# A 12-block transformer kernel with its instruction order written out by hand: new order, new counts of constant products, waits and weight loads moved

## The chip, the cores and the metric

The kernel runs on one core of one Trainium2 chip. The time is device time in microseconds (us) of one execution. The engines are PE (TensorE, matmuls; its weight loads are listed as PEld), DVE (VectorE), ACT (ScalarE), POOL (GpSimd) and SP (SyncE, which only waits and issues DMAs here). Each engine runs its own instructions in order; engines signal one another by semaphores.

## What is computed

Tokens x are 64 sequences of 64 rows by 128 columns; a context is 64 sequences of 128 rows by 96 columns. Four layers each add three blocks to x, every one on a normalised copy of x:

```
x = x + _L0_xattn_ref(_layernorm(x), ctx_768, ...)     # L0x: cosine scores against the context
x = x + _L0_attn_ref(_layernorm(x), ...)               # L0a: linear attention and a GELU MLP
x = x + _L0_ffn_ref(_layernorm(x), ...)                # L0f: 16 experts, 4 picked
x = x + _L1_xattn_ref(ctx_768, _layernorm(x), mask..)  # L1x: attention to context and latents
x = x + _L1_attn_ref(_layernorm(x), ...)               # L1a: 16 heads, rotary positions
x = x + _L1_ffn_ref(_layernorm(x), ...)                # L1f: MLP with 8 LoRA experts
...                                                    # L2x, L2a, L2f, L3x, L3a, L3f
```

L2x and L3x are attention with 16 heads to the context, L2a linear attention, L2f latent attention and 8 experts, L3a a gated linear attention and an MLP, L3f 8 experts of which 2 are picked, and a shared one.

## The kernel before

The tokens stay in SBUF (x_held, 32 tiles of 128 rows). A job is one block on a group of 4 tiles (2 tiles in L1x and L2f). Two contexts, each with its own 4 PSUM banks, semaphores and SBUF rooms, work through a list of jobs each (`PLAN`); each has one main job, and beside it the early part (norm, context tiles) of its next one.

Each block is written as Python generators, one for each engine (`pe_L2x`, `dve_L2x`, ...); what stands between two `yield`s is a step. `ORDER` is one long string that says in which order the steps are written out, and so the order of every engine's instructions. A lower-case letter is a step of context 0, an upper-case one of context 1: p, c, m, n are steps of PE; a, b, k, x, y of ACT; v, r, d, w, z of DVE; g, l of POOL; q, s of SP. A digit in front of a PE step is a number of constant products: `pe_warm` (line 456) writes as many products of two constants into a PSUM bank that is free at that point, and nobody reads them. `write_out` goes through the string. After each step it looks whether both contexts have written out their last job of the block three back; then it writes a wait of SP for those jobs (line 3048) and the DMA of the next block's weights (line 3009), since there are three weight rooms. All DMAs (weights, context tiles on line 518 and 1133, the experts' combination weights on lines 821 and 836) are on SP's queue.

Steps that the change touches:

- `j.free(v)` is DVE's wait for the end ("done") of its context's job before. In most blocks the first DVE step is this wait, and for a block's first job a memset.
- `pe_context` (L2x and L3x) projects the context to keys (line 1856) and values (line 1860), turns the normalised x and projects the queries (line 1870). Its last step only waits: for the queries (q_ready), the values in SBUF (va) and the keys, one plane for each lane (kx). PE's scores follow in `pe_waves` (L1a, L3x; line 1559) or in L2x's lanes (line 1953), which have those waits too.
- `dve_route_L3f` has a step that waits for e_low, which is written by the step before it.

Of the kernel before, what the change touches and what calls it, by code (L numbers as in the profile page):

```python
# [19 lines left out]
SLOTS = 3  # L20
# [761 lines left out]
def dve_L0a(nc, j):  # L782
    v, m, x = nc.vector, j.m, j.x
    yield
    j.free(v)
    if j.first:
        v.tensor_copy(m["va"][:, :, :, D], bcast(j.c["parity"][:, 0:2], 1, j.tiles))
# [522 lines left out]
def dve_L1x(nc, j):  # L1310
    v, m, x, psum = nc.vector, j.m, j.x, j.psum
    keys = SC + S
    yield
    j.free(v)
    if j.first:
        v.memset(m["vl"][64:P], 0.0)
        v.memset(m["plT"][64:P], 0.0)
    yield
    j.begin(v)
# [169 lines left out]
def dve_L1f(nc, j):  # L1489
    v, m, x, psum = nc.vector, j.m, j.x, j.psum  # L1490
    yield
    j.free(v)
    if j.first:
        v.memset(m["pickT"][:], 0.0)
# [100 lines left out]
def pe_waves(nc, j, keys):  # L1595
# [149 lines left out]
def pe_L1a(nc, j):  # L1745
# [17 lines left out]
    t.wait_ge(*j.at("va", 1))  # L1763
    t.wait_ge(*j.at("kx", 2))
    t.wait_ge(*j.at("qx", 1))
# [46 lines left out]
def dve_L1a(nc, j):  # L1812
    v, m, x, psum = nc.vector, j.m, j.x, j.psum
    yield
    j.free(v)
    if j.first:
        v.memset(m["va"][:, :, :, WIDTH], 1.0)
        v.memset(m["top"][:], 0.0)
# [30 lines left out]
def pe_context(nc, j):  # L1849
# [21 lines left out]
    yield  # L1871
    t.wait_ge(*j.at("q_ready", 1))
    t.wait_ge(*j.at("va", 1))
    t.wait_ge(*j.at("kx", 2))
# [17 lines left out]
def dve_context(nc, j):  # L1892
    v, m, x, psum = nc.vector, j.m, j.x, j.psum
    yield
    j.free(v)
    if j.first:
        v.memset(m["va"][:, :, :, WIDTH], 1.0)
        if "top" in m:
            v.memset(m["top"][:], 0.0)
# [127 lines left out]
def dve_L2x(nc, j):  # L2027
    v, m, x, psum = nc.vector, j.m, j.x, j.psum
    yield
    j.free(v)  # L2030
    if j.first:
        v.memset(m["va"][:, :, :, WIDTH], 1.0)
# [47 lines left out]
def pe_L3x(nc, j):  # L2080
    t, m, psum = nc.tensor, j.m, j.psum
    yield from pe_context(nc, j)
    t.wait_ge(*j.at("qx", 1))
# [79 lines left out]
def dve_L2a(nc, j):  # L2163
    v, m = nc.vector, j.m
    yield
    j.free(v)
    if j.first:
        v.tensor_copy(m["va"][:, :, :, D], bcast(j.c["parity"][:, 0:2], 1, j.tiles))
    yield from dve_linear(nc, j, j.c["same8"], j.c["head8"], 16)
    yield  # L2170
    dve_project(nc, j, 3)
# [278 lines left out]
def dve_L2f(nc, j):  # L2450
    v, m, x, psum = nc.vector, j.m, j.x, j.psum
    tok = j.tok
    yield
    j.free(v)
    if j.first:
        v.memset(m["va"][:, :, 16], 1.0)
# [218 lines left out]
def dve_L3a(nc, j):  # L2675
    v, m, x, psum = nc.vector, j.m, j.x, j.psum
    yield
    j.free(v)
    yield
# [104 lines left out]
def dve_route_L3f(nc, j):  # L2784
# [10 lines left out]
    yield  # L2795
    v.wait_ge(*j.at("e_low", 1))
# [3 lines left out]
def sp_L3f(nc, j):  # L2800
# [41 lines left out]
    "VVVVd4ppgGaapVGpppaakPAppkPPPDvvdDddvpAAalPpAAvvaavaPvPPPpVVVdKPAK4PVvAVAVApvVvvv4PvVPvvgVVv8pVVVa2pVVgGpppDDVDaaPppaaLD"
    "kAKppvPPvpPaAApdddlGApappaPvPAPPPVdbpvrrVrpapparvPAppPPPPparrrrrrrrrrrrrrrBrvvcAAbpapRRRRRRRvpssppPkVVsssPRRAaPPPpAaVggg"
    "PAPRvRvVVRRRRcccPgAggPcccggccPARRRRVvRpCBaPPpSSdDddDDpppPAbrrLSSaSvDpGpaKapvrrrvrrrrGGpaGpCCvrrrrrrVVCGGppCCGrrrrCCaGCVr"
    "lp1PpcAbadDvvDDpssssLPaBPsAppPPPgggVDvPaAAPVRVPAPPPRRVRRRkAccPpRRRRRRRRVRRRRRRvgAPPgVPgCccccggccBASSSSSPvpPapGpdpGaAbCpC"
# [185 lines left out]
def write_out(core, flows, last, load_weights):  # L3031
# [57 lines left out]
```

## Time and profile before

| | us |
|---|---|
| median of 3 runs (lowest, highest) | 2873.68 (2862.74, 2876.07) |
| span of the profiled execution, first to last instruction | 2859.1 |
| PE busy in it | 2483.8 |
| DVE, ACT, POOL busy | 1723.1, 1393.0, 782.2 |
| constant products on PE | 231.3, in 828 |
| TensorE clock granted, mean of full | 0.941 |

The profile gives the span of its execution and no total of its own. Busy times are a union over instructions; an engine that is not busy waits, or is between instructions. The granted clock is 1.00 at 2.4 GHz and 0.50 at 1.2 GHz, and a stretch's number is the mean over both.

### The profile page before, as it was taken

The page shows a single profiled execution, that of the slowest core. Times are in us where ns is not written, and L with a number is a line of the kernel's source. Part 1 is how long each engine was busy: PE and PEld are TensorE (multiplying, and loading weights), DVE is VectorE, ACT ScalarE, POOL GpSimd, SP SyncE. Part 2 cuts the span into 40 slices and gives each one's busy share as a digit, 9 for nine tenths or more (in the row PEclk, how much of TensorE's full clock was granted, in tenths as well). Part 3 has the DMA queues.
Part 4 walks back from the last instruction along what each step waited for, and adds up shares of the span by engine and source line. Part 5 has one row for each costly group of instructions (what it writes and reads, how often), then busy time and mean ns, then how long its engine had stood idle before and what let it go on. Part 6 is the DMA issues. An engine that isn't in the chain of part 4 may idle for free.

```text
span 2859.1 us, 63716 instructions
## 1 busy us (share of the span) xinstructions
PE 2483.8 (87%) x27260; PEld 1654.6 (58%) x27260; DVE 1723.1 (60%) x4680; ACT 1393.0 (49%) x2375; POOL 782.2 (27%) x684
## 2 busy tenths in 40 slices
PE   5899898887888899888998888788879888899999
PEld 3565566565555455455676666666545555566666
DVE  5766666656665657777676666555546555554533
ACT  3665345665443237676754344443334545654332
POOL 3322444543121231111012222221110022235444
PEclk9999999998889999999999898988979999899999
DMA  3001342000000001000000000000020000022133
GB/s 114 13 1 42 84 97 57 17 17 7 3 2 6 1 17 38 12 13 1 10 14 17 17 17 17 24 22 15 10 68 7 7 1 2 1 58 84 53 93 100
DMA packets 50459, 84.25 MB, mean 29 GB/s; under 512 B 9536, under 2 KB 24768, under 8 KB 49792
## 3 DMA queue, kind: packets, MB, share of 16 engines
q1 hardware_dynamic: 50176, 80.18, 10.2%
q8 instruction: 214, 3.51, 0.5%
q14 instruction: 69, 0.57, 0.1%
HBM read 77.54 MB, written 2.62 MB: 28 GB/s over the span
## 4 chain that ended last, share of the span: by engine, by line
PE 60%; DVE 17%; ACT 10%; issue 6%; POOL 5%; DMA 1%; SPq 0%; DVEq 0%; POOLq 0%; ACTq 0%
PE psum L917 5%; PE psum L875 4%; PE psum L879 4%; PE psum L456 3%; PE psum L1569 3%; PE psum L448 3%; PE psum L1559 2%; PE psum L1961 2%; PE psum L1953 2%; PE psum L1656 1%; POOL c_L3f_h L864 1%; DVE c_L3x_most L1698 1%; PE psum L2307 1%; PE psum L1856 1%; PE psum L1413 1%
## 5 line engine op out<-in xcount | busy, mean ns | idle before, releaser
L456 PE MATMUL psum<-halves_held 128*128 128x512 bf16 x828 | 231.3, 395 | 2.9 <-DVE c_L2x_p L2064 1.3
L907 DVE TENSOR_TENSOR c_L3f_h<-c_L3f_h,psum 128x512 f32<-128x512 f32 (+1 forms) x112 | 76.1, 685 | 115.5 <-PE psum L879 87.4
L864 POOL TENSOR_TENSOR c_L3f_h<-c_L3f_h,c_L3f_spread 128x512 f32<-128x512 f32 x96 | 121.5, 1299 | 85.9 <-DMA c_L3f_spread<-scratch 72.1
L456 PEld LDWEIGHTS psum<-halves_held 128*128 128x128 bf16 x828 | 77.1, 101 | 86.4 <-issue 31.2
L893 ACT ACTIVATE c_L3f_h<-psum 128x512 f32<-128x512 f32 (+1 forms) x112 | 65.2, 595 | 122.0 <-PE psum L875 99.5
L917 PEld LDWEIGHTS psum<-weights,c_L3f_h 128*128 128x128 f32 (+1 forms) x896 | 107.3, 193 | 17.8 <-issue 15.5
L917 PE MATMUL psum<-weights,c_L3f_h 128*128 128x128 f32 (+1 forms) x896 | 110.2, 278 | 0.2
L879 PE MATMUL psum<-c_L3f_xT,weights 128*128 128x512 f32 x208 | 106.1, 597 | 0.0
L875 PE MATMUL psum<-c_L3f_xT,weights 128*128 128x512 f32 x208 | 105.4, 596 | 0.0
L2058 DVE TENSOR_REDUCE c_L2x_mx<-psum 128x8 f32<-128x1024 f32 x64 | 77.6, 1219 | 43.3 <-PE psum L1953 42.9
L864 POOL TENSOR_TENSOR c_L0f_h<-c_L0f_h,c_L0f_spread 128x512 f32<-128x512 f32 x64 | 80.2, 1286 | 70.6 <-DMA c_L0f_spread<-scratch 59.1
L1698 DVE TENSOR_REDUCE c_L3x_most<-psum 128x16 f32<-128x2048 f32 x32 | 73.3, 2291 | 40.2 <-PE psum L1559 40.2
L1569 PE MATMUL psum<-c_L3x_qx,c_L3x_kT 32*128 32x256 f32 x512 | 77.6, 422 | 17.2 <-DVE c_L3x_most L1698 10.3
L2064 DVE SCALAR_TENSOR_TENSOR c_L2x_p<-psum,c_L2x_mx 128x1024 f32<-128x1024 f32 x64 | 77.7, 1220 | 1.3
L1997 ACT ACTIVATE c_L2x_p<-c_L2x_p 128x1024 f32<-128x1024 f32 x64 | 67.7, 1058 | 20.6 <-DVE c_L2x_p L2064 20.5
L1370 DVE TENSOR_TENSOR x_held<-x_held,psum 128x512 f32<-128x512 f32 (+1 forms) x48 | 28.6, 595 | 78.5 <-PE psum L2097 39.7
L1678 ACT ACTIVATE c_L3x_pT<-psum 128x1024 f32<-128x1024 f32 x64 | 62.7, 1020 | 26.0 <-PE psum L1591 25.7
L1953 PE MATMUL psum<-c_L2x_kx,c_L2x_qT 32*64 32x512 f32 x512 | 65.2, 625 | 11.5 <-DVE c_L2x_va L2039 6.9
L2002 ACT COPY c_L2x_pT<-psum 128x1024 f32<-128x1024 f32 x64 | 64.4, 1008 | 18.2 <-PE psum L1961 17.9
L1961 PE MATMUL psum<-constants_held,c_L2x_p 128*128 128x128 f32 x512 | 68.0, 276 | 5.5 <-ACT c_L2x_p L1999 5.3
L441 POOL TENSOR_TENSOR c_L3a_norm_rstd<-c_L3a_norm_rstd,constants_held 128x4 f32<-128x4 f32 x24 | 25.3, 1061 | 171.3 <-DVE c_L3a_norm_rstd L432 136.7
L917 PEld LDWEIGHTS psum<-weights,c_L0f_h 128*128 128x128 f32 x512 | 64.0, 203 | 13.8 <-POOL c_L0f_h L864 7.3
(645 smaller groups left out, 6822.0 us busy)
## 6 DMA issues: line engine op xcount, KB each, us to landing
c_L0f_spread<-scratch SPq DMA_DIRECT2D x64, 256.0 KB, 5.5
c_L3f_spread<-scratch SPq DMA_DIRECT2D x32, 512.0 KB, 5.6
c_L2f_spread<-scratch SPq DMA_DIRECT2D x64, 128.0 KB, 3.1
c_L3f_spread<-scratch SPq DMA_DIRECT2D x64, 128.0 KB, 5.9
c_L0x_ctxT<-ctxT SPq DMA_DIRECT2D x8, 384.0 KB, 7.6
c_L1x_ctx<-ctx SPq DMA_DIRECT2D x16, 192.0 KB, 2.4
c_L2x_ctxT<-ctxT SPq DMA_DIRECT2D x8, 384.0 KB, 3.9
c_L3x_ctxT<-ctxT SPq DMA_DIRECT2D x8, 384.0 KB, 4.0
```

Of the source, the lines that this page charges most:

```text
L448: put = nc.tensor.transpose(j.psum[0:width, bank, t * P:(t + 1) * P], x[:, t, :], j.c["ident"])
L456: nc.tensor.matmul(j.psum[:, bank, :], j.half["ident"], j.half["take"], start=True, stop=True)
L864: nc.gpsimd.tensor_tensor(h, h, j.m["spread"][:, f, :], ALU.mult).then_inc(*j.up("mixed"))
L875: t.matmul(psum[:, 1 + 2 * f % 3, 0:j.tok], j.weight("gate")[:, cols], m["xT"][:], start=True, stop=True).then_inc(*j.up("gate"))
L879: t.matmul(psum[:, 1 + (2 * f + 1) % 3, 0:j.tok], j.weight("up")[:, cols], m["xT"][:], start=True, stop=True).then_inc(*j.up("inner"))
L917: put = nc.tensor.matmul(j.psum[:, 0, k * P:(k + 1) * P], j.m["h"][rows, f, k * P:(k + 1) * P], j.weight("down")[rows, f * P:(f + 1) * P], ...
L1569: nc.tensor.matmul(j.psum[rows, g, at:at + 256].rearrange("p (j q) -> p j q", j=QUAD), j.m["kT"][f, s * keys:(s + 1) * keys], j.m["qx"][f, ...
L1698: put = v.tensor_reduce(m["most"][:, u, :].rearrange("p (g j) -> p g j", j=QUAD), psum[:, :, u * QUAD * keys:(u + 1) * QUAD * keys].rearra ...
L1953: put = t.matmul(psum[64 * r:64 * r + 64, g, :].rearrange("p (j k) -> p j k", j=QUAD), m["qT"][f, s * S:(s + 1) * S], m["kx"][f, :, s * SC ...
L1961: put = t.transpose(psum[:, n // 4, (n % 4) * P:(n % 4 + 1) * P], m["p"][:, n * P:(n + 1) * P], j.c["ident"])
L2058: v.tensor_reduce(mx, s, AX, ALU.max).then_inc(*j.up(lane_name("max", h)))
L2064: v.scalar_tensor_tensor(p, s, -limit, bcast(mx, 2, SC), ALU.max, ALU.subtract).then_inc(*j.up(lane_name("low", h)))
```

## The change

Steps that hold only a wait are gone or joined to the step that needs them, the waits of `pe_context` and `pe_L1a` now stand in `pe_waves` ahead of the first scores, a "+" in the order says where a weight load is written out, and the order with its digits is another one. PLAN, the arithmetic and the tiles are as before.

```diff
 def dve_L0x(nc, j):
     v, m, x = nc.vector, j.m, j.x
-    yield
-    j.free(v)
     if j.first:
+        yield
+        j.free(v)
         v.memset(m["tT"][64:P], 0.0)
...
@@ def pe_waves
         if w:
             pe_warm(nc, j, 2)
             t.wait_ge(*j.at("att", w))
+        else:
+            if tiles == 1:
+                t.wait_ge(*j.at("q_ready", 1))
+            t.wait_ge(*j.at("va", 1))
+            t.wait_ge(*j.at("kx", 2))
+            t.wait_ge(*j.at("qx", 1))
         pe_scores(nc, j, w, keys)
...
@@ def pe_L1a
     yield
-    t.wait_ge(*j.at("va", 1))
-    t.wait_ge(*j.at("kx", 2))
-    t.wait_ge(*j.at("qx", 1))
     yield from pe_waves(nc, j, S)
...
@@ def pe_context
     t.matmul(psum[:, 1, :], j.weight("wq"), m["xT"][:], start=True, stop=True).then_inc(*j.up("queries"))
-    yield
-    t.wait_ge(*j.at("q_ready", 1))
-    t.wait_ge(*j.at("va", 1))
-    t.wait_ge(*j.at("kx", 2))
...
@@ def dve_route_L3f
-    yield
-    v.wait_ge(*j.at("e_low", 1))
     yield from dve_weigh(nc, j)
...
 ORDER = (
-    "QVDDDdLdDdldKkqqdvddlDDdDkppLDaaKgPpaPgpAGppAvvavPAGPPvvPVvdVddlpagpAaVVdVpakgppQqQPDVDDLDPAApvvKGavvvPAPPGPVVAdddlVppag"
+    "dddlQqPADdkdDDLDdpapapKPaDDvdDVggLGlpppvvAaPAPGPPvvdvVVkQqqppaaAVVDVdgpaKgpppPPvvadvdAAPAGlGPPPvvdkdDDVppDVdAaapapgpgpVd"
...
@@ def write_out
-        if loaded < len(BLOCKS) and all(flow.finished > ends.get(loaded - SLOTS, -1) for flow, ends in zip(flows, last)):
+        if letter == "+":
             for flow, ends in zip(flows, last):
                 if loaded - SLOTS in ends:
                     core.nc.sync.wait_ge(flow.context.sem("done"), ends[loaded - SLOTS] + 1)
             load_weights(loaded)
             loaded += 1
+            continue
...
```

The same joining of `yield` and `j.free(v)` with `if j.first` is made in dve_L0a, dve_L1x (which keeps the wait in its second step), dve_L1f, dve_L1a, dve_context, dve_L2x, dve_L2a and dve_L2f; dve_L3a loses its wait, and pe_L3x its wait for qx, which is now in pe_waves. The first of the order's 71 lines stands above, old and new.

## Rows read from the trace of the kernel before

**Rows 1.** The page: span, busy time by engine, share of the ending chain.
```profile
span 2859.1 us, 63716 instructions
PE 2483.8 (87%) x27260; PEld 1654.6 (58%) x27260; DVE 1723.1 (60%) x4680; ACT 1393.0 (49%) x2375; POOL 782.2 (27%) x684
...
PE 60%; DVE 17%; ACT 10%; issue 6%; POOL 5%; DMA 1%; SPq 0%; DVEq 0%; POOLq 0%; ACTq 0%
```

**Rows 2.** Busy time by stretch: L0a, L1x, L1a, L2x, L2f, L3x/L3a, L3f.
```profile
core 0: us, PE busy (x) PEld busy (x) DVE busy (x) ACT busy (x) POOL busy (x), PEclk, DMA share, GB/s
120.00:290.00 170.00, 161.16 (x899) 107.08 (x898) 107.45 (x383) 102.81 (x170) 42.07 (x38) 1.00 0.10 23
450.00:660.00 210.00, 172.76 (x1705) 125.35 (x1704) 131.33 (x401) 134.24 (x338) 101.01 (x74) 0.98 0.07 20
660.00:930.00 270.00, 220.48 (x4163) 143.36 (x4159) 169.75 (x425) 118.93 (x197) 53.46 (x43) 0.88 0.02 4
1090.00:1420.00 330.00, 294.50 (x3684) 174.01 (x3683) 238.37 (x435) 240.87 (x316) 40.81 (x25) 0.97 0.03 8
1550.00:2080.00 530.00, 446.58 (x7076) 335.52 (x7075) 320.17 (x925) 214.59 (x373) 124.44 (x155) 0.90 0.06 17
2080.00:2500.00 420.00, 355.13 (x4488) 224.88 (x4487) 222.90 (x554) 206.82 (x319) 72.84 (x60) 0.91 0.05 15
2500.00:2859.00 359.00, 348.30 (x2048) 230.16 (x2046) 161.28 (x425) 143.85 (x238) 153.91 (x122) 0.99 0.28 77
```

**Rows 3.** Line 456: its group, its durations (min/median/max ns), and in L0a.
```profile
L456 PE MATMUL psum<-halves_held 128*128 128x512 bf16 x828 | 231.3, 395 | 2.9 <-DVE c_L2x_p L2064 1.3 <-DVE x_held L1370 1.0 <-DVE x_held L1529 0.6
...
L456 PE MATMUL psum<-halves_held x828: 377/379/634, 98.6 to 2465.9; 128*128 128x512 bf16 x166
...
120.00:290.00 170.00, 16.50 (x65) 6.11 (x65) 1.00 0.10 23
```

**Rows 4.** The chain that ended last, whole span, by line.
```profile
by line: issue 5.8%; PE psum L917 5.2%; PE psum L875 4.3%; PE psum L879 4.1%; PE psum L456 3.1%; PE psum L1569 2.8%; PE psum L448 2.6%; PE psum L1559 1.9%; PE psum L1961 1.6%; PE psum L1953 1.5%; PE psum L1656 1.2%; POOL c_L3f_h L864 1.2%; 
```

**Rows 5.** PE's waits, whole span: us in total, times, longest us.
```profile
PE psum L2295 <- ACT c_L2f_p L2378: 23.8, 19, 3.0
PE psum L535 <- DMA c_L0x_ctxT<-ctxT: 22.8, 1, 22.8
...
PE psum L1856 <- DMA c_L3x_ctxT<-ctxT: 9.9, 1, 9.9
...
PE psum L1953 <- DVE c_L2x_va L2039: 6.9, 3, 3.0
...
PE psum L448 <- DVE c_L2x_va L2039: 2.8, 1, 2.8
```

**Rows 6.** Around 2103 us: SP's and PE's timeline, the chain, DMA issues, busy time.
```profile
2103.41 0.37 SPq L3009 DMA_DIRECT2D weights<-weights  x1
2103.82 1.57 SPq L518 DMA_DIRECT2D c_L3x_ctxT<-ctxT  x3
...
2113.80 3.75 PE L1856 MATMUL psum<-c_L3x_ctxT,weights 96*128 96x512 f32 x4 [9.94 <-DMA c_L3x_ctxT<-ctxT]
...
2102.84 0.02 DVEq L2513
...
2102.91 0.43 DVE x_held L2514
...
weights<-weights SPq DMA_DIRECT2D x1, 2628.0 KB, 8.9
c_L3x_ctxT<-ctxT SPq DMA_DIRECT2D x3, 384.0 KB, 10.8
...
2114.00:2131.00 17.00, 15.92 (x135) 7.79 (x135) 10.15 (x22) 5.54 (x10) 1.25 (x2) 0.82 0.09 24
```

**Rows 7.** PE's timeline at 1156 us, with the idle time before.
```profile
1156.00 0.63 PE L448 MATMUL psum<-constants_held,c_L2x_att 128*128 128x128 f32 x4 [2.79 <-DVE c_L2x_va L2039]
```

More of the change, by code:

```diff
@@ L783, in dve_L0a @@
     v, m, x = nc.vector, j.m, j.x
-    yield
-    j.free(v)
     if j.first:
+        yield
+        j.free(v)
         v.tensor_copy(m["va"][:, :, :, D], bcast(j.c["parity"][:, 0:2], 1, j.tiles))
@@ L1312, in dve_L1x @@
     keys = SC + S
-    yield
-    j.free(v)
     if j.first:
+        yield
+        j.free(v)
         v.memset(m["vl"][64:P], 0.0)
@@ L1318, in dve_L1x @@
     yield
+    j.free(v)
     j.begin(v)
@@ L1490, in dve_L1f @@
     v, m, x, psum = nc.vector, j.m, j.x, j.psum
-    yield
-    j.free(v)
     if j.first:
+        yield
+        j.free(v)
         v.memset(m["pickT"][:], 0.0)
@@ L1813, in dve_L1a @@
     v, m, x, psum = nc.vector, j.m, j.x, j.psum
-    yield
-    j.free(v)
     if j.first:
+        yield
+        j.free(v)
         v.memset(m["va"][:, :, :, WIDTH], 1.0)
@@ L1893, in dve_context @@
     v, m, x, psum = nc.vector, j.m, j.x, j.psum
-    yield
-    j.free(v)
     if j.first:
+        yield
+        j.free(v)
         v.memset(m["va"][:, :, :, WIDTH], 1.0)
@@ L2028, in dve_L2x @@
     v, m, x, psum = nc.vector, j.m, j.x, j.psum
-    yield
-    j.free(v)
     if j.first:
+        yield
+        j.free(v)
         v.memset(m["va"][:, :, :, WIDTH], 1.0)
@@ L2164, in dve_L2a @@
     v, m = nc.vector, j.m
-    yield
-    j.free(v)
     if j.first:
+        yield
+        j.free(v)
         v.tensor_copy(m["va"][:, :, :, D], bcast(j.c["parity"][:, 0:2], 1, j.tiles))
@@ L2452, in dve_L2f @@
     tok = j.tok
-    yield
-    j.free(v)
     if j.first:
+        yield
+        j.free(v)
         v.memset(m["va"][:, :, 16], 1.0)
@@ L2842 @@
[L2842 to L2845, printed above, removed]
@@ new lines @@
+    "LlVqQdDVkvKQDvPAPAaPAPvDvvGGPPVVdDALDVVVdpapapgagKppPAPpAPAPdDDDlLvvavdlLGGPPvVDVkAvpaK3pvVvvaaaVdvvD1pkKdVPAddvVDD+pvDv"
+    "vPVvVAAAvVvV9PvlgvlLgpVPVVVdVVdVVGLVGappapaappppPakpvvApkPaAPAPpDvvaaaAdDvdvPAKPPpPPvVVPpAPvvVVAVvAAKVPvvdvvVPgvlDdVVVVl"
+    "DVVDVgGVLGLd1pappppaappPaappvvAkkPpPPaAAAPPPpDdvdvPAPKaavDvdVVaPpvAPVVAAAldKkVpVvvvvvvvg7PVPv1pVa2ppppapVVVVVVlGVDDDLDLD"
+    "daaPpGgpaAPpAPAKvvpPPAaAPPpvvaaakvvdPPdVVPpvAPVVKAAAVVpvPdvvvvVvPvgDVvVVVVDVVGlDdV7pappppapaapPpkaApPLGgDvvpPPPaAAAAPpPb"
@@ new lines @@
+    "PPprrKadrVdrrrrrVrrPppAPPprvPpBaARrRRRdrRRrRvrrrRrrRappprPcRRVAbPPAaRDRRRRDRPRRVPvRCPABsslpapvdpapsSsSS+SSsvDVpgcvVggLDc"
+    "PPcpPpkKAaaAGgGCcvVgggGPVcpvGgGPcccvpaCpGCbrrrrrrrrrrrrrrpPPpCpAavrrappCarVrrvrPcpbpaAGddvVGpCCpCvpVPpaAssgcssPgscpvpPPB"
+    "aRRRRRdRRRvRRRRRAPAaRRRRPpppgldVvRRRCPBkAaggggccccDvVgPccPAPvVDdVSSGpaGSCpCSSbrdrrrrrrrGPppPPCrrrrAapPrVDdrPrrrvaAVPApPr"
+    "rLDrcpGPabCKAvpvVVlGGGCCppaCpGsssgCvVgggpPcaAPcsBvdRRRPpPpcRRRRDRRRRaAcgcpvRRRVRRRRsRRPpPCappAkBaVvvggccPgPPcAVvPpaSSGCG"
@@ new lines @@
+    "SqSpCAbGPPVDPAPppCpDGVaPprrrdrrrdrrArrrrvrrrSPCVPpGLdDGrAVrrrrcbaPldCaAvVCpGCpKvaGCppssggdVDDvPsgaApcPcBDRvdRssQRRRRdRRR"
+    "RpcaRRRgRgLDRRpRDvRRpcpcPaKpakvldRDgPCBpgvPcAVcgPcAkvdDVSSGPpPpAaapPCppqSSSAaaLdvdaPGvDVdGlgVvgvdPACPCPPvVddPAKGgPVvvpAa"
+    "VDppPaaAkPpdlGGCVvvaGGCCCCvvV+PpVvDdVPAPPaApAkAaPApGDDVdLDvvGdVVGVVppappapPPPagaagAAAPqQvdvvgDdDVVDvv9pppAaaaKVlLdVPdDdp"
+    "dVvvAKPAPladVDDvvPAPPpPAkAakAPAQvVdDDGVGpa2pVVvpapppaaaLGvVDDVgvdpagvvDPPAAPAPVDVdqgdv8pAVVp2PLldvVdpKAaaaPApPDKvVVDvddP"
@@ new lines @@
+    "PAPPAPaAkAAlDDvdvpDvGGVVVakpapGdvvddqQdVVLlDDDppaapagvDdLdDdpPPPaAAApPVdVaKAkgvvlgdVVd9PvVv1pkAKapPAapPVDaPpPvvVAAPaAPPA"
+    "AvvpvGVGapa2pVVDDDvGVLDVqQppapaapPPPpAaAAPdDDvgdvDdLVVKaAgDvvVVglvvd8PVDKA2pppaaaPpddvvdkAPVVlPPAAPPPaAAAdDvvdDpvDakpapG"
+    "GLVVDVvdGVqQVDdvppapaagDdlddvDpPPPAAAapPVVaKAgLvvgVVvD9PVdv1ppkAKaPaApaPVDDPApDvdvPAPPaAAPADvldvVpvGGLVakpapVVGvDVdVqQdd"
+    "DppapaaKpPPPAgAAapPavDvVDgLVAvvVgVdvvDl9PdV1pppAaaakPApPKdDdvdldvVPPAPPAPaAAAVDvvDpvGGVQakpapVDVGVVLDDvdDvDppaappPPPpagK"
@@ new lines @@
+    "AAAaPLvDVVaAgvvdVVg9PvVvdA2paKpPAapPVDaPPpAPAVDvvdDlAaPAPADLGVvvGdVV7pGvapakVVpvPPAPpAAPa1ppvddVVvvvAVdVvp9PggvVvDvApaPA"
+    "5PKpVVv+PA7PPpvVV2papPVVapPapVlgGGAVVdPVa2pvVGvP1PpAPAAPPvDvppAa1PpVVPkaappa5pDVVDvvPPA2pPaAApPLvddpPaApPpDvVVdvvvgglPAK"
+    "2PpVPA2PapDvDvvVpvPvVdp1papPapapPVgGDVVVGVAPa4pVVvPPvpLvvGAPAAPPp1pAaPpVDVPVVkaappa2pvvPp1PaA1pPvpAaAPppPvvvAKpPvgVVPA5P"
+    "gapdvvvVpPA2PvdvppPapPapapa6pPDVVDDVVGVVvvdV4pgGGlvdvAPVVp1pakpPaa2PppAaP1pvvAPApPapAPvdddVVpappvvvvp4PvVpPggLlavvpgVDvv"
@@ new lines @@
+    "4PAPAppaAPpPapaApPapVVvdv2pPKAPvVvpPAp2PaPpPkaappa5pVVVGVVVVvvGApaPP1pVVvpaPPpvvvDvAPaaAAPPvvvvvvvvvvvvvvvvpAPapvdvVvVPv"
+    "VdvVppaPpPpAapPvDvDdgLglGpAaAaPPAppPvDVvVKggppPApPV+DdPpAkPAvVVvVVvpAaV8pVVVVVVVVVVVVvVVVvPAPaVVvVaDVvvvvvPAPvvVdvvvvPvd"
+    "VvvvAPPvpvvGPAapPVvvVGAPPppDGLdVDGvPPaPpVVVvKapPApPVvVVgaAAlgppapVVDVVVVvVVVvDVdVVVggppppVVVvVVvVvPkpAaPpaVvdVvvaPPAvvPP"
+    "APvDvvvvdvvvvvvvvVvVLGGpPAaPpAPVvvVvvDPPGPKGPVdVvVPApPpVDVaAVDAVDVVapppVVVVVVVVVVVVVvPvLggVlpAapVvPapDVvdVppgpgpPkAvvPVP"
@@ L2911 @@
+    "PAPPpVpPAaPVPAvVAPPPVPAPAVPAVPVPPPcpppaAaAVvvVgggssSSSSSgggGGGGgggGGGgGGGGGcccccccccccccCCCCCCCCCCCCCvCVsS")
 class Flow:
@@ L3050, in write_out @@
             loaded += 1
-    assert all(flow.finished == len(flow.jobs) for flow in flows)
+            continue
+        flow = flows[letter.isupper()]
+        flow.step(letter.lower(), warm)
+        warm = 0
+        flow.open()
+    assert loaded == len(BLOCKS) and all(flow.finished == len(flow.jobs) for flow in flows)
 BLOCKS = ["L0x", "L0a", "L0f", "L1x", "L1a", "L1f", "L2x", "L2a", "L2f", "L3x", "L3a", "L3f"]
```

119 lines of the change are left out of this document (44 added, 75 removed).

## The prediction

> **What bounds the kernel now.** I read the page first. The matmul engine is busy 87% of the span and no other engine more than 60%, and PE carries 60% of the chain that ended last [rows 1]. So time is won in two ways: by taking work off PE, or by filling the moments in which PE waits for another engine. The table by stage shows which stage wants which. From 2500 us on (L3f) PE is busy 348 of 359 us: only less PE work would help, and the change removes none there. From 1550 to 2500 us (L2f, L3x, L3a) PE is idle 148 of 950 us, and from 660 to 930 us (L1a) 50 of 270 us; these stages also have the low granted clocks, 0.88 to 0.91 [rows 2]. Over the span the mean clock is 0.941. With levels of 1.2 and 2.4 GHz that is (1 - 0.941) x 2 = 12% of the span, 337 us, at 1.2 GHz.
>
> Part of what keeps PE busy is no work of the reference: the constant products on line 456, 828 of them, 231.3 us, or 0.279 us each [rows 3]. They stand ahead of a wait and occupy PE while it would wait. If they last longer than the wait, they are on the path: the chain puts 3.1% of the span on them, 89 us [rows 4]. So about 89/231 = 0.385 of their time sets the end.
>
> PE's own waits are many and short: the longest total is 23.8 us in 19 waits. One is different: 9.9 us at a single place, for the context tile of an L3x job [rows 5].
>
> **Part 1, weight loads in the order.** In the kernel before, SP waits until both contexts have finished L2f, and then sends the 2,628 KB load for L3f (2103.41 us); the three ctxT transfers for L3x stand behind it on SP's queue and land a median 10.8 us after issue. PE ended its matmuls at about 2103.8 and starts L1856 at 2113.80, 9.94 us idle, released by that DMA [rows 6]. In the new order I followed the letters by job: the transfers for L3x groups 1 and 5 stand ahead of the "+" of L3f's weights, and group 1's stands ahead of the last L2f job's end. What held it was SP's queue. The tile's own condition is an older job of its context. What is late next is the L2f job's "done" (x_held, line 2514, 2102.91 plus 0.43 us), on which L1856 also waits, so it could start at about 2103.9. I take -10 us; bounds 0 (another SP wait ahead of it takes its place) and -13: behind the gap the clock is 0.82 for 17 us [rows 6], which is 6 us at the lower level, half of it lost. The other eight loads stand near their old places by my count of steps (within some 30 of 8,000), but for L1a's, which now stands behind L0f's first spread transfers, and has over a thousand steps before its weights are used: 0.
>
> **Part 2, waits moved.** L2x and L3x jobs had a PE step that only waits (q_ready, va, kx). PE runs in order, so everything behind it waits too. L2x's lanes carry the same waits themselves. Counted in the old order, in two of eight L2x jobs this step stands ahead of the lanes with a PE step of the other context between; in L1a the moved waits stand one such step ahead of the scores in two jobs of eight, in L3x in none. The trace shows one such: at 1156.00 the transposes of another job's att waited 2.79 us for DVE's c_L2x_va [rows 7], which they do not read. The step's waits are in the groups L1953 <- va 6.9 us and L448 <- va 2.8 us [rows 5]. I take -3; bounds 0 and -9.7. DVE loses some 70 waits, nearly all on "done"; it is idle 40% of the span [rows 1] and the next instruction waits for later work of the same job anyway. I take 0: the cover is DVE's idle time, and without it each would cost an instruction's start, the 0.02 us of "DVEq" pieces in the chain ahead of line 2514, so under 2 us in all. That a step with memsets now exists only for a block's first job changes nothing that runs.
>
> **Part 3, fewer constant products.** The digits of the order add up to 828 before and 655 after: 173 fewer. By block: L0a 84 to 31, L1x 147 to 95, L2x 265 to 203, L2f 101 to 77, L2a 33 to 15, L1f 13 to 8; more in L1a (57 to 74) and L3x (101 to 127); L3a 26 to 25, L0f 1 to 0. PE's work falls by 173 x 0.279 = 48 us. Where a product filled a wait, the wait comes back, and nothing is won. With the chain's share: 48 x 0.385 = 19 us. Bounds: 0 and -48. I take -19, since the stages that lose most have their PE busy 82 to 95% [rows 2] with the products in it.
>
> That counts the clock as unchanged. A constant product takes a median 379 ns and at most 634 ns [rows 3]; 1.67 is the price of the lower level on this shape. The Trainium skill (TensorE: Matmul & The Clock Gate, "What's actually happening") says that the throttled state is the default and activity releases it; this speaks against removing filler. The same page ("HAM oscillation — how this bites in real kernels") charges half of the time at the lower level. The rows bear the rule out only loosely: L0a with 5% idle has 1.00, L1a with 18% idle has 0.88 [rows 2].
>
> **Part 4, the order of the rest.** Following both orders step by step, PE's sequence is nearly kept: in most blocks a PE step has moved past less than 1.5 steps of the other context on average; L0f, L2x and L3f more (3 to 5). DVE's have moved past 1 to 5, ACT's past up to 2.4. The contexts' jobs are the same. So this is a local reshuffle. What it can win is PE's waits: 375 us idle in all, of which the start (22.8 us for the first ctxT) is untouched. What it can lose is of the same kind: an ACT or DVE instruction placed behind one that waits. The nearest rows are the single waits of 1 to 4 us behind the groups of [rows 5]. I take -5, bounds +30 and -40, a tenth of PE's idle time up and down.
>
> Sum: -10 - 3 - 19 - 5 = -37 us, on the profile's span 2859.1: 2822. The page gives no total for that execution; the runs' median 2873.7 lies 14.6 us above the span, which I carry over: 2837 us, 1.3% less.
>
> **Rivals.** *A larger gain.* The products removed were nearly all overrun, and the new places fill waits: -10 - 3 - 48 - 20 = -81, 2793 us. For it: the counts rise exactly in L1a and L3x, where the clock is 0.88 and 0.91 [rows 2]; if L1a alone rose to 1.00, 65 us at the lower level x 0.82 busy x 0.40 = 21 us would be won. Against it: the chain puts only 89 us on all 828.
>
> *No change to speak of.* The moved waits come back elsewhere and the removed products had filled waits: -13 alone, 2861 us. For it: most of the chain's pieces are single instructions of three engines handing on, and a changed order trades one wait for another.
>
> *Slower, by the clock.* The stages around L0a, L1x and L2x (120:290, 450:660, 1090:1420, 710 us, mean clock 0.98) lose 167 products and fall to L1a's 0.88. That is 710 x 0.10 x 2 = 142 us more at 1.2 GHz; PE is busy 0.885 of it, and by 1 - 379/634 [rows 3] loses 40%: +50 us. With -13 from parts 1 and 2: 2911 us. It decides from a loss of 27 us, a fall of 5 to 6 points. By the half that the Trainium skill's page on TensorE charges it would be +63 and 2924, an estimate. Against it: L0a has 5% idle including 16.5 us of products [rows 2, 3], so without the 53 (15 us) it is still 86% busy, as L2f's and L3a's stages at 0.9 are, and that is also what speaks for it.
>
> **How the numbers follow.** Forecast (2815 to 2859): 0.47. Larger gain: 0.17. No change: 0.19. Slower: 0.17. About 0.5%, 14 us, is what a measurement of this kernel can tell from none. The range 2790 to 2895 leaves out the far half of each outer case, under 2 in 10. Faster than 2859: 0.64; within 2859 to 2888: 0.19; slower: 0.17. The forecast's own range is 2815 to 2859.
>
> **What would show it.** Part 1: no PE wait for c_L3x_ctxT, and the ctxT transfer issued before the 2,628 KB load. Part 2: no L448 released by c_L2x_va. Part 3: line 456 x655, near 183 us busy, PE idle up by less than 48 us, chain share near 2.5%. The clock rival shows as a granted clock under 0.95 in 120:290 or L1x's and L2x's stages; the prediction fails if the mean clock leaves 0.93 to 0.96, or if PE's idle total grows by as much as its work falls.

## The result, and the profile after

The changed kernel takes 2752.4 us (median of 4; 2751.4 to 2761.7) against 2874.9 us before: ratio 0.959, 95% interval 0.957 to 0.961. I had forecast 2837 and a range that ended at 2790. The sign was right, the size a third of what came.

The page of the kernel after, span and busy time:

```profile
span 2752.2 us, 63312 instructions
PE 2412.4 (88%) x27087; PEld 1615.5 (59%) x27087; DVE 1664.2 (60%) x4680; ACT 1388.0 (50%) x2371; POOL 779.1 (28%) x684
```

Beside [rows 1]: PE busy 71 us less and PE idle 35 us less (375 to 340), together the span's 107. Line 456, its group and its durations:

```profile
L456 PE MATMUL psum<-halves_held 128*128 128x512 bf16 x655 | 192.9, 405 | 7.5 <-DVE c_L2x_p L2064 7.5
...
L456 PE MATMUL psum<-halves_held x655: 376/379/634, 105.5 to 2370.2; 128*128 128x512 bf16 x164
```

38 us less than in [rows 3]. So 33 us of PE's fall are no removed product: the same matmuls of the reference occupied PE for less time. The mean granted clock rose from 0.941 to 0.955, which is (0.059 x 2 x 2859) - (0.045 x 2 x 2752) = 337 - 248 = 89 us less at the lower level. By the prices that the prediction's clock rival used (PE busy 0.87 of the time, 40% lost at the lower level, from 379 and 634 ns) these 89 us are 31 us of PE time, an estimate that comes out at the 33.

Where in the kernel? An instruction that each job has shows how far it has come: ACT's copy of the turned x (xT), one or more in each job. Its rows give the first and the last start; first the kernel before, blocks L0f, L2x, L2a, L2f, L3x, L3a, L3f:

```profile
L464 ACT COPY c_L0f_xT<-psum x8: 570/586/587, 239.6 to 409.6; 128x512 f32<-128x512 f32 x8
...
L464 ACT COPY c_L2x_xT<-psum x16: 563/586/603, 1071.0 to 1404.3; 128x512 f32<-128x512 f32 x16
...
L464 ACT COPY c_L2a_xT<-psum x16: 582/586/593, 1407.2 to 1486.1; 128x512 f32<-128x512 f32 x16
...
L465 ACT ACTIVATE c_L2f_xT<-psum,weights x32: 455/474/492, 1484.0 to 2069.2; 128x256 f32<-128x256 f32 x32
...
L464 ACT COPY c_L3x_xT<-psum x16: 570/586/592, 1940.4 to 2421.2; 128x512 f32<-128x512 f32 x16
...
L465 ACT ACTIVATE c_L3a_xT<-psum,weights x24: 668/777/779, 2259.4 to 2653.4; 128x512 f32<-128x512 f32 x24
```

and the same of the kernel after:

```profile
L464 ACT COPY c_L0f_xT<-psum x8: 583/585/587, 246.6 to 415.3; 128x512 f32<-128x512 f32 x8
...
L464 ACT COPY c_L2x_xT<-psum x16: 558/585/607, 1070.4 to 1395.0; 128x512 f32<-128x512 f32 x16
...
L464 ACT COPY c_L2a_xT<-psum x16: 585/585/596, 1397.7 to 1473.1; 128x512 f32<-128x512 f32 x16
...
L465 ACT ACTIVATE c_L2f_xT<-psum,weights x32: 456/473/489, 1472.8 to 1999.0; 128x256 f32<-128x256 f32 x32
...
L464 ACT COPY c_L3x_xT<-psum x16: 569/585/592, 1885.1 to 2325.3; 128x512 f32<-128x512 f32 x16
...
L465 ACT ACTIVATE c_L3a_xT<-psum,weights x24: 687/777/777, 2165.8 to 2545.1; 128x512 f32<-128x512 f32 x24
```

Up to L0f the new kernel is 6 us behind, at the first L2x job level, at the last L2a job 13 us ahead. Then L2f wins 57, L3x 26, L3a 12 us. Of the three blocks that lost most of the products, L0a (53) and L1x (52) won nothing, and L2x (62) about 9 us (first to last copy 333 us before, 325 after). From L2f on the order has as many products as before, 229 for 228 (by its digits): all of the 173 fewer lie ahead of the stages where the gain is. The windows between these marks show how (columns as in [rows 2]); kernel before, L2f and L3x:

```profile
1486.00:2069.00 583.00, 491.19 (x7902) 371.45 (x7901) 354.59 (x1025) 239.89 (x420) 138.94 (x172) 0.91 0.06 19
2069.00:2421.00 352.00, 300.22 (x4030) 185.29 (x4026) 185.77 (x451) 165.72 (x261) 47.12 (x40) 0.91 0.06 17
```

and after, L0a, L1x, L2x, then L2f and L3x:

```profile
120.00:290.00 170.00, 144.97 (x818) 98.97 (x816) 101.36 (x381) 99.76 (x170) 43.02 (x39) 0.99 0.12 27
450.00:660.00 210.00, 164.70 (x1592) 123.34 (x1593) 125.36 (x398) 128.75 (x323) 99.44 (x72) 0.93 0.07 20
1090.00:1420.00 330.00, 290.58 (x3685) 172.47 (x3684) 238.76 (x460) 246.64 (x326) 39.82 (x26) 0.98 0.03 8
1473.00:1999.00 526.00, 457.97 (x7877) 351.10 (x7881) 348.97 (x1033) 229.84 (x412) 140.31 (x174) 0.96 0.07 21
1999.00:2325.00 326.00, 294.68 (x4067) 184.16 (x4053) 183.81 (x452) 165.09 (x258) 46.86 (x40) 0.95 0.05 18
```

In L2f PE's busy time fell by 33 us, of which 24 products fewer are 7, its idle time by 24 (92 to 68), and the clock rose from 0.91 to 0.96. In L0a, where products left, PE's idle time rose from 9 to 25 us [rows 2].

The place that part 1 spoke of, SP's timeline after:

```profile
2015.65 12.79 SPq L518 DMA_DIRECT2D c_L3x_ctxT<-ctxT  x2
2028.53 0.37 SPq L3003 DMA_DIRECT2D weights<-weights  x1
```

The transfer for group 1 goes out 13 us ahead of the weight load, and no 9.9 us wait [rows 5, 6] is left among PE's waits, whose largest totals now are

```profile
PE psum L535 <- DMA c_L0x_ctxT<-ctxT: 20.7, 1, 20.7
PE psum L1231 <- DVE c_L1x_p L1353: 19.4, 8, 4.9
```

Line numbers of the changed code differ a little from those before: its 1860 is the projection to keys, 1856 before, and its weight load stands on line 3003 (3004 in runs with a longer order).

### The profile page after: what moved, and what is told of

The parts are those of the page before. It is cut to its first block, busy times and chain, and to the rows that moved or that the text cites. A ratio compares the mean times of both kernels' runs of the same rounds, so it can differ in the third digit from the quotient of the medians.

```text
span 2752.2 us, 63312 instructions
## 1 busy us (share of the span) xinstructions
PE 2412.4 (88%) x27087; PEld 1615.5 (59%) x27087; DVE 1664.2 (60%) x4680; ACT 1388.0 (50%) x2371; POOL 779.1 (28%) x684
## 4 chain that ended last, share of the span: by engine, by line
PE 57%; DVE 21%; ACT 10%; issue 6%; POOL 4%; DMA 2%; SPq 1%; DVEq 0%; POOLq 0%; ACTq 0%
PE psum L917 6%; PE psum L879 4%; PE psum L875 4%; PE psum L1570 3%; PE psum L456 3%; PE psum L448 2%; PE psum L1560 2%; PE psum L1961 2%; PE psum L1663 1%; PE psum L1953 1%; DVE c_L3x_most L1705 1%; PE psum L1364 1%; PE psum L1414 1%; DVE c_L2x_mx L2058 1%; PE psum L1415 1%
## 5 line engine op out<-in xcount | busy, mean ns | idle before, releaser
L456 PE MATMUL psum<-halves_held 128*128 128x512 bf16 x655 | 192.9, 405 | 7.5 <-DVE c_L2x_p L2064 7.5
L456 PEld LDWEIGHTS psum<-halves_held 128*128 128x128 bf16 x655 | 60.4, 102 | 85.3 <-issue 35.5
L2016 POOL TENSOR_TENSOR c_L2x_kx<-c_L2x_kT,constants_held 128x1024 f32<-128x1024 f32 x16 | 32.6, 2060 | 197.1 <-ACT c_L2x_kT L1882 197.1
L864 POOL TENSOR_TENSOR c_L2f_h<-c_L2f_h,c_L2f_spread 128x256 f32<-128x256 f32 x64 | 45.3, 732 | 120.4 <-DMA c_L2f_spread<-scratch 118.7
L1961 PEld LDWEIGHTS psum<-constants_held,c_L2x_p 128*128 128x128 f32 x512 | 58.6, 144 | 34.6 <-issue 23.9
L1460 POOL TENSOR_TENSOR c_L1f_hT<-c_L1f_hT,c_L1f_r 128x512 f32<-128x512 f32 x32 | 40.7, 1274 | 116.6 <-DVE c_L1f_hT L1518 116.5
L917 PE MATMUL psum<-weights,c_L0f_h 128*128 128x128 f32 x512 | 69.0, 285 | 4.7 <-POOL c_L0f_h L864 4.5
```

Of the source, the lines that this page charges most:

```text
L456: nc.tensor.matmul(j.psum[:, bank, :], j.half["ident"], j.half["take"], start=True, stop=True)
L864: nc.gpsimd.tensor_tensor(h, h, j.m["spread"][:, f, :], ALU.mult).then_inc(*j.up("mixed"))
L917: put = nc.tensor.matmul(j.psum[:, 0, k * P:(k + 1) * P], j.m["h"][rows, f, k * P:(k + 1) * P], j.weight("down")[rows, f * P:(f + 1) * P], ...
L1961: put = t.transpose(psum[:, n // 4, (n % 4) * P:(n % 4 + 1) * P], m["p"][:, n * P:(n + 1) * P], j.c["ident"])
```

## The experiments

All but e2 and e6 are the changed code with a string made from the two orders: every step keeps its job, and only its place and its digit are chosen. Where an experiment mixes, a step goes ahead of another whenever both original orders have it so; otherwise the place wished for decides. Each diff below is the first place at which its string differs. Ratios are to the kernel before, run beside it, with their 95% interval. Runs that did not stand in one comparison are set against each other by these ratios, times 2870 us.

**The parts by themselves.** e1 against the changed kernel's code has the old order; e2 the new order with the old digits; e3 the old order with the new digits; e4 moves one "+" of e1.

```diff
 # e1: e4 moves the "+"
-CCCvapaV+GlQQqvPvApDVVPvPA5
+CCCvapaVGlQQ+qvPvApDVVPvPA5
 # the changed kernel: e2
-aaaVdvvD1pkKdVPAddvVDD+pvDvvPVvVAAAvVvV9PvlgvlLgp
+aaaVdvvD8pkKdVPAddvVDD+pvDvvPVvVAAAvVvV8PvlgvlLg7p
 # e1: e3
-aVvvaaKv8pdVV+dKDdPVvllpADddkkDLLvvvPVvVAAAVVvvvg8PDDvg7
+aVvvaaKv1pdVV+dKDdPVvllpADddkkDLLvvvPVvVAAAVVvvvg9PDDvgp
```

> The changed code with the old order of all steps, the old 828 constant products at their old places and the weight loads where they were; only the steps that held nothing but a wait are gone. Theory 'order' (the gain of 122 us is made by the new sequence of steps): ratio 0.997 to 1.002. Rival 'waits' (the waits that stood in steps of their own were the cost): ratio under 0.985.

Measured: 2861.7 us, ratio 0.996 (0.993 to 0.999), a hair outside the window of the theory and far from the rival's. The moved waits are worth 4 in a thousand, 11 us.

> The changed kernel with the old number of constant products (828) ahead of each step. Theory 'order': most of the gain stays, about 2770 to 2785 us (the 173 products more cost at most 48 us on PE). Rival 'counts' (products removed, or placed where the clock had fallen, made the gain): 2840 us or more.

Measured: 2822.0 us, 0.983 (0.978 to 0.988), between the two theories. The new order keeps under half of the gain with the old digits.

> The old order with the new 655 products. Theory 'order': 2850 to 2880 us, since the counts were fitted to waits that stand elsewhere in this order. Rival 'counts': 2790 us or less. My forecast's term for the counts alone was -19 us: 2855 us.

Measured: 2904.7 us, 1.010 (1.005 to 1.016), above the windows of theory and rival. The new digits in the old order cost 1.4% over e1; in the new order they win 2.4% (e2 against the change). So the new counts have no worth of their own.

> As e1, but the 2,628 KB load of L3f's weights is issued behind the context transfers of L3x groups 1 and 5. Both theories: the 9.9 us wait of PE for that transfer shrinks to the landing time of a lone transfer, about 4 us after its issue, so 5 to 10 us less than e1. Rival 'SP wait': nothing, since SP gets to the transfers only when the last L2f job is done, as before.

Measured: 2843.8 us, 0.990 (0.986 to 0.994): 0.6% less than e1, 18 us by the ratios, with intervals that just touch; the wait that is gone was 10 us. The rest may be the scatter of executions: the profile of e4 is 14 us ahead of e1's at the last copy of L0f (412 and 426 us) and 8 us shorter in L2f, both ahead of the moved load, where the two run the same instructions. The rival "SP wait" fell: SP gets to the transfer 18 us ahead of the load, as its timeline shows:

```profile
2084.21 0.33 SPq L518 DMA_DIRECT2D c_L3x_ctxT<-ctxT  x1
2085.20 2.53 SPq L836 DMA_DIRECT2D c_L2f_spread<-scratch  x4
2087.77 14.69 SPq L518 DMA_DIRECT2D c_L3x_ctxT<-ctxT  x2
2102.55 0.37 SPq L3004 DMA_DIRECT2D weights<-weights  x1
```

**The parts by stage and by engine.** e5 is old up to L2a's end and new behind it; e6 the reverse; e7 and e8 are e1 with one engine's steps moved from L2f on, and with what must move along.

```diff
 # e1: e5
-AlPdvvV+papvKaPvvApPvVDDDvAPlgggLpdPpAAkkVVV
+AlPdvvV+aapPpvvVvvA1PVvAPPpAgggVVGppppvvPvVA
 # the changed kernel: e6
-vD1pkKdVPAddvVDD+pvDvvPVvVAAAvVvV9Pvlgvl
+vD1pkKdV+PAddvVDDpvDvvPVvVAAAvVvV9Pvlgvl
 # e1: e7
-papvKaPvvApPvVDDDvAPlgggLpdPpAAkkVVVDppGLvDKKPvv
+papvKaPvVvAvpPVvAPlgggpPpAVVAppGvvPvVapaPvVapVG
 # e1: e8
-AlPdvvV+papvKaPvvApPvVDDDvAPlgggLpdPpAAkkVVVDppG
+AlPdvvV+appvKaPvvAPvVpDDDvAPPlgggLpdpAAkkVVVppDG
```

> The old order and counts up to the end of L2a, the new order and the new counts from L2f on, L3f's weight load as in the change. Theory 'late order' (the profile after gained nothing up to the last L1f job and 13 us up to L2a's end, so the gain is made behind it): ratio 0.960 to 0.970. Rival 'whole' (old and new parts only fit together): 0.98 or more.

Measured: 2768.6 us, 0.966 (0.963 to 0.970), as the theory had it.

> The new order and counts up to the end of L2a, the old ones from L2f on. Theory 'late order': ratio 0.990 to 0.998 (the 13 us up to L2a's end). Rival 'whole': other than that, e.g. 1.00 or more.

Measured: 2873.5 us, 1.001 (0.998 to 1.004), over the window of "late order": the first half of the new order wins nothing by itself. The 13 us up to L2a's end in the profile after are less than single profiles scatter: the profiles of the runs that share the old first half and its digits (e1, e4, e5 and e7 to e16) have their last L2a copy at 1481 to 1505 us. e6's is at 1495.1, the profile after has 1473.1. Steps and digits are the same in these two up to there, but e6's weight loads of the first half, L1a's above all, stand where they stood before, and no run tested these places.

> As e1 (old order, old counts, old loads), but from L2f on DVE's steps wish for their new places: of 4035 pairs of DVE steps that the change turns round, 3501 are turned; of PE's 1850, 310; of ACT's 1430, 706, as many as keep each step behind those it needs. Theory 'DVE' (what holds PE in L2f is DVE and ACT work behind work that is not urgent): 30 us or more off e1, about 2830 us. Rival 'PE' (the sequence of PE itself): within 10 us of e1.

Measured: 2995.0 us, 1.045 (1.042 to 1.048), 4.9% over e1. The theory "DVE" fell, and not in the direction of its rival.

> As e7, but PE's steps wish for their new places: 1115 of PE's 1850 pairs turned, 227 of DVE's 4035, 116 of ACT's 1430. Theory 'DVE': within 10 us of e1 (2862 us). Rival 'PE': 30 us or more off it.

Measured: 2980.7 us, 1.039 (1.036 to 1.043). "PE" fell too. The windows of L2f in e7, then e8:

```profile
1491.50:2149.00 657.50, 513.01 (x7901) 385.13 (x7901) 350.98 (x1024) 241.32 (x418) 138.42 (x172) 0.88 0.06 17
```

```profile
1485.00:2140.00 655.00, 526.50 (x7903) 395.39 (x7901) 355.59 (x1025) 243.13 (x422) 139.25 (x172) 0.86 0.06 17
```

Against L2f's window of the kernel before, PE's idle time rose from 92 to 145 and 129 us, and its busy time with the falling clock (0.91 to 0.88 and 0.86) from 491 to 513 and 527, with the same 7,901 weight loads. Both mixtures turn only a part of the pairs that the change turns, so they say what these two mixtures cost, not what one engine's order is worth.

**Order, counts, load and products from L2f on.** e9 is e5 with the old digits, e10 is e5 with the load ahead of the transfers, e11 and e12 are e1 and e5 without a product from L2f on.

```diff
 # e5: e9, and e12 (the same place)
-PpvvVvvA1PVvAPPpAgggVVGppppvvPvVAapPvVaap
+PpvvVvvAPVvAPPpAgggVVGppppvvPvVAapPvVaapp
 # e5: e10
-ppPAqSSSQVvVdpavpvvGGGGgpCaC1paCCCvpVPADVvdvPQ+qPpA2PAVD
+ppPAqSSS+QVvVdpavpvvGGGGgpCaC1paCCCvpVPADVvdvPQqPpA2PAVD
 # e1: e11
-PvVAvAgv3pPaVPpparVVrrvppPPvVVbpPparrrA
+PvVAvAgvpPaVPpparVVrrvppPPvVVbpPparrrAv
```

> As e5 (new from L2f on), but with the old counts of constant products everywhere: only the order is new, and only from L2f on. Theory 'order frees PE': within 15 us of e5, 2770 to 2785 us. Rival 'counts raise the clock': half or more of e5's gain gone, 2820 us or more, and a mean clock near 0.94.

Measured: 2789.2 us, 0.973 (0.968 to 0.978), a few us beyond the theory's window. Against e4, which has the old digits and the load moved too, the order from L2f on is worth 1.7%, 49 us (32 to 67 by the intervals); the new digits there 0.65%, 19 us (e9 to e5; the intervals of the two overlap a little), with 229 products for 228, so by their places and not by their number. L2f's window in e4, then in e9:

```profile
1487.40:2067.80 580.40, 481.37 (x7884) 366.23 (x7908) 353.21 (x1030) 241.72 (x424) 140.54 (x174) 0.93 0.06 19
1481.10:2009.90 528.80, 452.48 (x7884) 346.78 (x7909) 345.69 (x1031) 229.54 (x412) 140.70 (x174) 0.98 0.07 21
```

With the same matmuls and the same number of products PE is idle 23 us less (99 to 76) and busy 29 us less, at 0.98 instead of 0.93. (e9's profile is of its fastest execution.)

> As e5, but L3f's weight load is issued ahead of the context transfers of L3x groups 1 and 5, as before the change. If the place of this one load is worth in the new order what e4 against e1 showed in the old one: 10 to 20 us more than e5, 2780 to 2790 us, and PE's 10 us wait for the transfer is back. Rival: nothing, since the new order has other PE work to put there.

Measured: 2776.1 us, 0.969 (0.965 to 0.972), 6 us over e5 by the ratios, less than the theory's 10 to 20 and not clear of noise. The wait is back:

```profile
PE psum L1860 <- DMA c_L3x_ctxT<-ctxT: 9.9, 2, 9.7
```

> The old order (as e1) without any constant product from L2f on (228 of 828 left out; they are part of no result). It tells what the products are worth. Theory 'clock': without them the granted clock from 1500 to 2500 us falls under 0.88 and the time rises by 30 us or more over e1, to 2890 or more. Rival 'filler costs': 2840 us or less, since 228 x 0.3 = 68 us of PE work is gone.

Measured: 2893.9 us, 1.010 (1.007 to 1.013). "Filler costs" fell: 228 products less on PE and 40 us more than e1 by the ratios. The clock from 1500 to 2500 us is 0.86, where e1 has 0.91, as the theory "clock" had it.

> As e5, without any constant product from L2f on. Theory 'order frees PE': the gap to e11 stays 70 us or more, so the order's gain does not hang on the products. Rival 'the new counts do it': the gap shrinks to under 40 us.

Measured: 2813.8 us, 0.983 (0.977 to 0.988), 80 us less than e11, which stood beside it. e12 has the load behind the transfers too, which is worth 6 to 18 us of this (e10, e4). With no product on either side the order keeps its gain. L2f's window in e11, then in e12:

```profile
1503.00:2103.00 600.00, 485.87 (x7783) 379.47 (x7783) 353.51 (x1025) 240.53 (x420) 138.64 (x172) 0.86 0.06 18
```

```profile
1488.00:2033.00 545.00, 462.61 (x7777) 360.51 (x7775) 347.90 (x1024) 228.86 (x408) 139.84 (x173) 0.91 0.07 21
```

This is the cleanest pair: nearly the same matmuls, no filler. The order takes 32 us off PE's idle time (114 to 82), and PE's busy time falls by another 23 us with the clock going from 0.86 to 0.91. By the clock alone, (0.14 x 2 x 600) - (0.09 x 2 x 545) = 70 us less at the lower level, of which PE is busy 0.82 and loses 40%: 23 us, an estimate that comes out at what was measured. Part of this pair is scatter: the two profiles lie 94 us apart, the medians 80.

**Which steps.** In the new order the norm steps of the next job (d, l, k) stand later in the string, by 46, 61 and 88 places on average from L2f on (counted in the two strings); routing and down steps (r, b, s, c) earlier, by 5 to 15. In the mixed strings the moves are a little smaller.

```diff
 # e1: e13
-vvV+papvKaPvvApPvVDDDvAPlgggLpdPpAAkkVVVDppGLvDKKPvv
+vvV+papvaPvvApPvVvAPgggpPpAAVVVppGvPvvapVaPvVapVGpGv
 # e1: e14
-v3pPaVPpparVVrrvppPPvVVbpPparrrAvrrrrpaPAPvpppVrrrra
+v3pPaVPprrpaVrVvppPbPrrrvVVpPpaArrrrrrrrcvpaPAbPsssv
 # e1: e15
-AlPdvvV+papvKaPvvApPvVDDDvAPlgggLpdPpAAkkVVVDppGLvDK
+AlPdvvV+aapPpvKvVvvAPVvAPPpDDDAglggVVLGpdpppvvPvVAkk
 # e1: e16 (new order in L2f alone)
-AlPdvvV+papvKaPvvApPvVDDDvAPlgggLpdPpAAkkVVVDppG
+AlPdvvV+aapPpvvVvvAPVvAPPpAgggVVGppppvvPvVAapPvV
```

> Old order, old counts and old loads as e1, but from L2f on the steps of the next job's early part (d on DVE, l on POOL, k on ACT: the norm of x) stand at their new, later places, on average 37, 49 and 80 steps later in the string; PE's sequence is left nearly alone (97 of 1850 pairs turned). Theory 'late norms' (norm steps written too early block DVE, ACT and POOL for steps that PE waits for): 2825 us or less, at least half of the late order's gain. Rival 'routing': within 10 us of e1 (2862).

Measured: 2901.9 us, 1.014 (1.009 to 1.019), 1.8% slower than e1. "Late norms" fell as a cause by itself, and it was not "within 10 us", as its rival had it.

> As e1, but from L2f on the routing steps (r on DVE, b on ACT, s on SP) and the down products (c on PE) stand at their new, earlier places, 2 to 6 steps earlier on average. Theory 'routing' (combination weights that come earlier let the down products fill PE's waits): 20 us or more off e1. Rival 'late norms': within 10 us of e1.

Measured: 2890.8 us, 1.009 (1.005 to 1.012), 1.2% slower than e1. "Routing" fell as well.

> The complement of e13: old counts, from L2f on all steps at their new places (PE's sequence entirely: 1841 of 1850 pairs) but for d, l and k of the next job, which stay about where they were. Theory 'late norms': under half of the late order's gain over e1, 2835 us or more. Rival: the main steps carry it, 2815 us or less.

Measured: 2848.6 us, 0.991 (0.987 to 0.994), 0.6% off e1, but level with e4 (0.990). In e15 one of the transfers for L3x goes out 13 us ahead of the weight load (2070.1 and 2083.1 us), and no wait of PE for them is left, so what e15 wins is as much as the load's place wins alone. PE's new sequence entire, with the norms at their old places, wins nothing more that shows. Its window of L2f:

```profile
1481.00:2053.00 572.00, 483.12 (x7866) 369.51 (x7896) 353.33 (x1024) 229.42 (x412) 139.69 (x173) 0.91 0.07 20
```

Idle 89 us and clock 0.91, as before the change (92 and 0.91): without the norms' later places PE's waits do not shrink in L2f.

> Old order, the new one inside L2f (up to the end of both contexts' last L2f job), old order again behind it; old counts and the load as in the old order. By the stages of the profiles, L2f's stretch was 57 us shorter after the change: 2805 to 2820 us if the gain is made there and adds up by stages; 2850 or more if the stage only shifts waits into the next.

Measured: 2804.4 us, 0.978 (0.972 to 0.984), 1.8% off e1, 53 us. The load is not quite where it was: in the new order of L2f a transfer for L3x goes out ahead of it, and PE's 10 us wait is gone here too.

```profile
2058.24 0.59 SPq L518 DMA_DIRECT2D c_L3x_ctxT<-ctxT  x1
2071.00 0.36 SPq L3004 DMA_DIRECT2D weights<-weights  x1
```

So the order in L2f is worth 35 us against e4 (1.2%; 15 to 55 by the intervals), of the 49 for all stages from L2f on. L2f by itself carries most of the order's gain, and it stays in the stages behind.

## Why the forecast was wrong

**The step that failed is part 4, "the order of the rest"**, -5 us with bounds of +30 and -40. It measured -49 us from L2f on, beyond its bound, at the same counts and the same place of the load (e9 against e4), and e16 puts 35 of it into L2f. I had counted how far steps moved and taken "nearly kept" for "little won", and had taken a tenth of PE's idle time with no row behind it. That PE's sequence is nearly kept was true and said nothing: PE's new sequence with the old places of the norms wins no more than the load's place does (e15 and e4), the norms alone cost 1.8% (e13), and mixtures that follow one engine's sequence 4 to 5% (e7, e8). Cut at L2f's two ends the order keeps most of its worth (e5, e16); cut by engine or by role it loses it. My reading is that each engine's place for a step has to match the places of those that feed it and wait for it. The mixtures agree with that; no run shows it at a single step.

**The second error is in the same sum: a won wait was priced once.** I held the clock fixed. In L2f 32 us of removed idle time came with 23 us less busy time for the same matmuls (e11 to e12), with TensorE at 2.4 GHz for more of the stretch. The Trainium skill (TensorE: Matmul & The Clock Gate, "What's actually happening") says activity releases the throttle. The pair agrees, with idle 114 to 82 us and clock 0.86 to 0.91. I had used the clock in two rivals, once for products that were added and once for products that left, and never for waits that close. That the clock made the 23 us rests on its size, which the price from 379 and 634 ns gives, and on executions of the same instructions, where it can be seen with no wait removed. From the start to the last copy of L0f e4 and e1 are the same code; their profiles, e4's first, show

```profile
0.00:412.20 412.20, 348.36 (x1912) 225.89 (x1923) 265.83 (x869) 199.29 (x344) 135.18 (x119) 0.96 0.22 55
0.00:426.00 426.00, 366.36 (x1912) 234.11 (x1923) 266.20 (x869) 199.51 (x344) 134.86 (x119) 0.92 0.21 54
```

with PE's idle time alike (64 and 60 us) and the same work of DVE, ACT and POOL; but PE is busy 18 us more where the clock is 0.92 instead of 0.96. (0.08 x 2 x 426) - (0.04 x 2 x 412) = 35 us more at the lower level would be 12 by the same prices, so these are rather low. And over the 51 executions of the kernel before that ran beside the experiments the granted clock goes from 0.927 to 0.946 and the time from 2891 to 2850 us, a fitted 18.5 us for each 0.01, where the same prices give 0.01 x 2 x 2870 x 0.87 x 0.40 = 20. What sets the clock of an execution at the start is not known, and no run was made to vary it.

**Part 3, the counts,** was put at -19 us with the clock unchanged. As one number it was ill-posed: the same digits are worth +40 us in the old order (e3 against e1), about -19 us from L2f on (e9 to e5), where their sum is not lower at all, and -69 us in the whole new order (e2 to the change). The reasoning from "3.1% of the chain over 231 us" missed that in L0a the products had filled waits: 38 fewer in its window (9.8 us), and PE idle 16 us more. With the old digits in the new order, on the other hand, the last copy of L0f starts at 444.5 instead of 415.3 us, and from L1f's last to L2x's last it is 36 us more (397 against 361). These are single profiles, and in this first half profiles of one order lie up to 24 us apart (under e6). Nor do fewer products mean less time: 228 fewer cost 40 us (e11). Line 456's own readings came as forecast: 655, 2.5% of the chain, 193 us against my 183.

**Part 1, the load,** -10 us: the mechanism is as predicted, PE's wait of 9.9 us is gone in the change and in e4 and back in e10. Its size lies between 6 us (e10 to e5) and 18 us (e1 to e4), each known to some 15 us either way.

**Part 2, the waits,** -3 us with a bound of -9.7: 11 us (e1; 3 to 19 by the interval). In e1 the 2.8 us wait of L448 for c_L2x_va is gone, and those of L1953 for it are 4.9 us instead of 6.9. The rest of the 11 was not traced.

**The rivals.** "A larger gain" had the sign and a price of 81 us, 37 less than came; it put the surplus on the products. "No change to speak of" fell. "Slower, by the clock" fell as a whole: the clock went from 1.00 to 0.99 in L0a and from 0.97 to 0.98 in L2x. But its sign stands in L1x, where the clock fell from 0.98 to 0.93, under the 0.95 that I had named: 62 products fewer in that window are 15.2 us, and PE is busy only 8 us less. By the rival's own prices a fall of 0.05 over 210 us costs 7 us, an estimate. So that mechanism seems to have been at work in one stage of three, and L2f's gain covered it.

**Its own time.** I carried 14.6 us from span to median. The run that belongs to the span after is 1.3 us longer than it (2753.5 and 2752.2), and the kernel before varied from 2850 to 2891 us between executions of the later comparisons. So 1.3 of the 14.6 us were time around the span and the rest that spread.

The terms as measured, each by ratios x 2870: waits -11 (e1), load -18 (e4), order from L2f on -49 (e9), digits there -19 (e5), and from e5 to the change -21 for the new first half with its digits and load places. They are steps of one row of runs, so that their sum is the ratio's -118 says nothing for them. The last is not additive: nearly the same first half before the old second half is 0.5% slower than e1 (e6).

What stays open: which steps of L2f must move together, and what made the last 21 us. e7, e8 and e13 to e15 show that none of these mixtures, each by an engine or a role, is enough; no run found a small set that is.

## What to carry to other kernels

When an order is searched as a whole, look at the idle time of the bounding engine by stage; here about a quarter of L2f's went (99 to 76, 114 to 82). How far the steps moved told nothing. Price a closed gap on PE twice, once as a wait and once as clock, in a stretch whose granted clock is under 1.00: in L2f the second part was 23 to 29 us beside 23 to 32 of the first. Fillers such as constant products are part of the order they were counted in: after a reordering count them again, and do not judge them by their sum. Check in each mixed run what else came along: in e15 and e16 a transfer went ahead of the load with the moved steps, and 10 us of PE's waits with it.

## What the runs showed that I had not expected

A wrong mixture costs more than the right order wins: 140 us over e1 (e7) against 49 us, with every engine's work the same to within a few per cent.

The order also changes ACT's work. Loads of activation tables in L2f's stretch before, then after, by line:

```profile
L893 ACT ACT_TABLE_LOAD x22 | 28.2, 1283 | 0.4
L2346 ACT ACT_TABLE_LOAD x11 | 14.1, 1283 | 0.2
L2378 ACT ACT_TABLE_LOAD x9 | 11.5, 1283 | 0.2
```

```profile
L893 ACT ACT_TABLE_LOAD x18 | 23.1, 1283 | 0.3
L2345 ACT ACT_TABLE_LOAD x9 | 11.5, 1283 | 0.2
L2377 ACT ACT_TABLE_LOAD x7 | 9.0, 1283 | 0.1
```

Eight fewer at 1.28 us: ACT is busy 230 instead of 240 us there. This by itself is not what shortens L2f: e15 has the same 34 loads and 229 us, and its L2f takes 572 us.
